# cpe1's depthwise convolution and layer norm: TensorE's round reordered, its lags one block shorter

## The reference

```
t = img2tok(x)
t = t + img2tok(_dwconv(tok2img(t), cpe1_w, cpe1_b))     # 3x3 depthwise convolution, "cpe1"
shortcut = t
tn = _ln(t, n1_g, n1_b)                                  # layer norm over the 128 channels
act_res = jax.nn.silu(tn @ actproj_w + actproj_b)
ti = tn @ inproj_w + inproj_b
ti = jax.nn.silu(img2tok(_dwconv(tok2img(ti), dwc_w, dwc_b)))
```

## Time and profile before

| | |
|---|---|
| median of 3 runs | 3499.59 us (3496.89 to 3507.64) |
| the profiled execution: its time, its span | 3514.0 us, 3512.2 us |
| its granted TensorE clock, mean | 0.939 of 2.4 GHz |
| busy PE, DVE, ACT, POOL | 84%, 65%, 63%, 18% of the span |

### The profile page before, as it was taken

The page is one execution under the profiler, slowest core; times in us unless marked ns, Lnnn a source line. Parts: engine busy times, 40 slices in busy tenths (PEclk is TensorE's granted clock), DMA queues, the critical chain, the costliest instruction groups (busy, mean ns, idle before and its releaser), DMA issues. The chain is left out here.

```text
span 3512.2 us, 56298 instructions
## 1 busy us (share of the span) xinstructions
PE 2946.8 (84%) x18996; PEld 1552.5 (44%) x18996; DVE 2289.3 (65%) x2743; ACT 2212.2 (63%) x2537; POOL 645.5 (18%) x420
## 2 busy tenths in 40 slices
PE   3788877979988887798998887787998988788799
PEld 2344335335544433534554443443555444353355
DVE  5677656667468765577655965667756696475772
ACT  2787645557668754546767964554767777464474
POOL 0025200610003510060000540024000153004200
PEclk9999998989999999898999999998999999998899
DMA  2000556700110156570020015854002004476201
GB/s 66 22 1 15 147 144 175 178 14 0 63 37 1 41 125 171 152 173 10 0 81 19 0 55 130 223 142 113 9 14 85 0 0 121 120 200 163 60 0 54
DMA packets 158335, 274.52 MB, mean 78 GB/s; under 512 B 19844, under 2 KB 120903, under 8 KB 158151
## 3 DMA queue, kind: packets, MB, share of 16 engines
q1 hardware_dynamic: 158150, 272.02, 29.0%
HBM read 194.07 MB, written 77.88 MB: 77 GB/s over the span
## 5 line engine op out<-in xcount | busy, mean ns | idle before, releaser
L1007 PE MATMUL psum<-region,m_fc 128*128 (+1 forms) x768 | 294.2, 507 | 19.6 <-DVE region L1655 11.7
L273 DVE SCALAR_TENSOR_TENSOR region<-region,cols 128x768 f32<-128x768 f32 x288 | 292.9, 1017 | 22.8 <-DVE region L273 9.2
L729 POOL TENSOR_TENSOR region<-work,region 128x768 f32<-128x768 f32 x48 | 87.0, 1812 | 1017.6 <-DVE work L1627 1017.6
L1281 PE MATMUL psum<-work,m_fc 128*128 128x384 f32 x768 | 270.6, 486 | 0.0
L700 POOL TENSOR_TENSOR work<-work,region 128x768 f32<-128x768 f32 x96 | 174.5, 1817 | 505.5 <-DVE work L1448 505.5
L960 ACT ACTIVATE work<-psum,cols 128x768 f32<-128x768 f32 x192 | 173.0, 901 | 142.1 <-PE psum L1007 141.6
L1007 PE MATMUL psum<-work,m_avg 128*128 128x384 f32 x576 | 227.4, 519 | 15.1 <-ACT work L836 7.2
L1007 PE MATMUL psum<-region,m_cen 128*128 (+1 forms) x384 | 157.1, 535 | 88.1 <-DVE region L1508 49.9
L1518 DVE SCALAR_TENSOR_TENSOR work<-region,cols,work 128x768 f32<-128x768 f32 x192 | 200.6, 1045 | 11.5 <-DVE work L1518 5.2
L1007 PEld LDWEIGHTS psum<-region,m_fc 128*128 128x128 f32 x768 | 140.9, 195 | 148.3 <-ACT work L960 46.7
L681 POOL MEMSET region<- 128x98 f32 (+1 forms) x20 | 4.2, 209 | 1043.2 <-DVE region L1649 627.2
(11 more groups left out here) (236 smaller groups left out, 6895.3 us busy)
## 6 DMA issues: line engine op xcount, KB each, us to landing
work<-scratch_cpe SPq DMA_DIRECT2D x192, 196.0 KB, 4.0
work<-scratch_dwc SPq DMA_DIRECT2D x192, 196.0 KB, 4.1
work<-scratch_lepe SPq DMA_DIRECT2D x192, 196.0 KB, 3.9
region<-in_tab_ch SPq DMA_DIRECT2D x192, 192.0 KB, 3.8
region<-in_x SPq DMA_DIRECT2D x48, 384.0 KB, 3.3
region<-in_tab_tok SPq DMA_DIRECT2D x48, 384.0 KB, 3.2
out<-work SPq DMA_DIRECT2D x48, 384.0 KB, 2.3
scratch_cpe<-region SPq DMA_DIRECT2D x44, 392.0 KB, 4.3
```

The lines of the kernel that those rows point to most:

```text
L273: eng.scalar_tensor_tensor(out=tgt, in0=prow(k, b, *TAPS[n]), scalar=tap_weight(conv, TAPS[n]), in1=tgt, op0=ALU.mult, op1=ALU.add).then_i ...
L729: g.tensor_tensor(region_tile(3, 4 + p), tile(p), region_tile(3, 2 * p), ALU.mult).then_inc(f2_qc, 1)
L1007: last = pe.matmul(psum[:, bank + s, 0:HC], weights[:, :], moving(s), start=(n == 0), stop=(n == len(terms) - 1))
L1281: last = pe.matmul(psum[:, 4 + s, 0:HC], fc2[:, P * j:P * (j + 1)], static(tile(4 + j))(s), start=(j == 0), stop=(j == 3))
```

## The change

Three tables are written anew; no stage, wait or tile changes. Each engine's `cpe1_run`:

```diff
 # ScalarE
-                cpe1_run = [(0, cpe1_centre), (3, squares), (4, root)]
+                cpe1_run = [(0, cpe1_centre), (3, root), (2, squares)]
 # TensorE
-                cpe1_run = [(3, centre), (4, var), (1, convolve)]
+                cpe1_run = [(1, convolve), (3, var), (2, centre)]
 # VectorE
-                cpe1_run = [(5, normalise), (2, add_taps), (1, left), (1, right)]
+                cpe1_run = [(1, left), (1, right), (4, normalise), (1, add_taps)]
```

## The result

| | before | changed |
|---|---|---|
| median of the first runs | 3501.64 us (4 runs) | 3460.05 us (4 runs, 3452.18 to 3473.39) |
| ratio, first comparison | | 0.989, 95% interval 0.9862 to 0.9918 |
| profiled execution: span | 3512.2 us | 3459.4 us |
| its granted clock | 0.939 | 0.943 |

The kernel became 1.1% faster, 41.6 us by the medians; 3455.0 had been forecast.

What follows compares the result with a forecast made beforehand. A closed ring of dependences in cpe1, no engine, was taken as the bound: -36.1 (rounds), -18.0 (tail), +3.5 and +6.0 (head) make -44.6 us, from 3499.6 to 3455.0 us, range 3440 to 3472.

Steps and rivals of the forecast that it cites:

- The ring: cpe1's loop: normalise, centring, variance, root close in 6.03 us; reordered, they span two rounds, needing 7.1 of 9.76 us.
- TensorE as the next bound: cpe1's loop: TensorE then bounds rounds at 4.88 us, -36.1 us over eight rounds in four images.
- dwc as the model of it: dwc's similar rounds take 4.87 us with TensorE always busy, so register work and fetches were taken to add nothing.
- Rival 1: cpe1's loop: the fetches become the bound, 16 us of the gain go, 3471 us; chance 0.12.
- The upper bound of its price: Fetches in cpe1's rounds: at most 0.17 us for some six rounds an image, 0 to +4 us, taken as 0.
- The tail: From convolve(11) to the second in_act(1): shorter lags take out 4.5 us per image, -18.0 us in four.
- The head: Start of cpe1: add_taps(0) ahead of residual(10) delays l1_out(11), +3.5 us, and the lower clock adds +6.0 us.
- the term for the clock: Head of cpe1: the clock falls in all four images, two more than before at 3.0 us each, +6.0 us.
- Rivals 2, 3 and 4: Ring only moved, 3491 us, chance 0.05; clock stays down, 3533, 0.02; no clock fall in the head, 3443, 0.13.
- rival 4: Head of cpe1: no fall of the clock, first two images win 3.0 us each, 3443 us; chance 0.13.

Runs made afterwards that it cites:

- the repetition: The changed kernel run once more, against the kernel before: 3459.82 us (6 runs), ratio 0.9869.

## Why the prediction was right

**The ring.** Read from one round of the timeline, it is confirmed from several sides. With all orders changed the convolutions are 4.88 us apart in every image: 156.3 us for 32 rounds against 156.2 forecast (4 x 39.04). The three experiments that keep one or two engines in the old order each close another ring, of 5.6 to 12 us. The change is one thing in three tables; of the pieces tried, two cost 166 and 200 us by themselves, single runs, with the longer rounds in their traces.

**TensorE as the next bound, and dwc as the model of it.** That the loop's register work adds nothing and that the fetches keep up was taken from dwc's rounds; both hold. Rival 1 did not come: in cpe1 a single wait for a fetch was long enough to show in each of the two profiles of the changed kernel, 0.20 and 0.22 us. But it stood close, with fetches that landed 0.1 us ahead of their convolutions in the first rounds. The upper bound of its price, 5.05 us of packets a round, was too high a reading of the share: with the convolution shortened, the fetches did with 4.5.

**The tail.** -19.1 against -18.0; the first image alone gives 16.07 us against 16.2, and the other images were a little longer before than the first. The new tail was laid out rightly. What the prediction says of the difference, that the shorter lags took out the 4.5 us, is only partly so: measured from the kernel before, 1.4 to 1.7 us of an image's 4.6 to 4.9 are the lower clock after the pause of 2.95 us, which the new order doesn't have. The lags are worth 4.5 us against the new order with long lags, and that one's tail is 1.3 us longer than the old order's at full clock. The prediction weighed the clock in the head and left it out here; that its difference holds all the same is because it started from the measured 20.71.

**The head.** +6.5 against +9.5; the repetition has +8.2. Right, or nearly so: the pause of 3.99 us (3.9 forecast; l1_out(11) is 0.97 us later, not 0.87), and the clock below 1.00 after it in all four images here and in the repetition. Mis-sized: the term for the clock. It was taken at 3.0 us an image for two more images, with nothing more or less for the first two. From l1_out(11) to the first centring the four images now take 5.2, 6.0, 6.1 and 5.2 us, not 6.5. l1_out(11) took 1.91, 2.90, 2.90 and 1.61 us there, between the 1.53 of full and the 2.90 of half speed: in two images the stretch at half speed covers only a part of it, so the price of one is 1.7 to 2.6 us over the undisturbed 3.5. In the repetition it was 2.5 to 2.7 us, as worked out from the starts of convolve(0) and convolve(3). The warning of the Trainium skill against longer pauses ("TensorE: Matmul & The Clock Gate", Why this matters for your kernels) was to the point, in eight heads of eight.

**Rivals 2, 3 and 4** did not come: no engine waits for `rstd` in the first image's loop by more than 0.2 us, the clock is 1.00 in the rounds, and it fell in every head. The experiment with VectorE's runs a step later shows what rival 4 had at stake and more: with the pause gone too, 16 us.

Open: why the clock fell after 3.0 us in two images and not in two others (the same two in the kernel with TensorE's order alone), and after 2.3 us in two of four, while after 2.95 us in the tail of the kernel before it fell in all four. The length of the pause alone doesn't decide it. No experiment here changed the length or the place of one pause alone.

## What to carry to other kernels

Where several engines each run a fixed order of stages, look for the closed ring that gives the round its length: follow from one instruction what each next one waited for, its own engine's order among it, until it comes back one block later. Here the ring was opened only by the orders of all three engines together, and one engine's order alone closed a longer one, so every ring, the shorter ones too, has to be added up before a table is changed. Then look at the joint where one stage's run begins in another's end: an order that is right in the loop can put a wait ahead of the last blocks' work there.

## What I had not expected of the hardware

- A share of 1.0 of the DMA engines' time is not their limit. For the same mixture of fetches and stores it read 0.83 at 211 GB/s, 1.01 at 257 and 1.04 at 281.
- A pause costs twice. In the two kernels with one order changed, rounds computed at 9.9 and 9.4 us came out at 12.0 and 11.4, because TensorE paused some 4.2 to 4.9 us in each and came back at the lower of its two clock levels (a convolution of 4.09 us instead of 2.17).
- The length of a pause didn't decide alone whether the granted clock fell. In the heads it fell after 2.3 us in two of four, after 3.0 us in the same two of four in two profiles, after 3.99 us in 20 of 20 (five profiles), after 1.39 us in none of four. In the tails it fell after 2.95 us in four of four in one kernel, in two of four in another.
- VectorE and GpSimd slowed each other down where they ran at the same time: 3.50 us for a pair of tap instructions that takes 2.06 elsewhere, 2.57 for a multiplication that takes 1.80. That they did so by running side by side is read from the rows; no experiment moved them apart alone.
